# Attention in steps of four scores and about four maxima, each followed by a batch with V of at most four banks

## The reference

```python
t = _to_tokens(x)                      # 16 x 3136 x 32
Q, K, V = ln(t) @ W_Q, ln(t) @ W_K, ln(t) @ W_V
scores = einsum('bqd,bkd->bqk', Q, K) * 32 ** -0.5
probs = softmax(where(causal, scores, -inf), axis=-1)
t = t + einsum('bqk,bkd->bqd', probs, V)
```

## Time and profile before

| | |
|---|---|
| median of three runs (lowest, highest) | 4711.1 us (4706.0, 4712.6) |
| the profiled execution's own time | 4710.3 us |
| its span | 4708.6 us |
| TensorE matmul busy | 4141.0 us (88%), 51290 matmuls |
| VectorE busy | 3134.4 us (67%) |
| ScalarE busy | 2752.3 us (58%) |
| POOL busy | 1430.2 us (30%) |
| mean granted TensorE clock | 0.942 of 2.4 GHz |
| layer 2 attention, first score to end | 1597 to 2984 us |
| layer 3 attention, first score to end | 3168 to 4547 us |

### The profile page before, as it was taken

One profiled execution on the slowest core, in us unless ns is written; L12 is line 12 of the kernel. 1 busy time (PEld: TensorE's weight loads), 2 busy tenths in 40 slices (PEclk: granted clock), 3 DMA queues, 4 the chain that ended last, 5 costly groups with the idle time before them and its releaser, 6 DMA issues. The chain is left out here.

```text
span 4708.6 us, 125775 instructions
## 1 busy us (share of the span) xinstructions
PE 4141.0 (88%) x51290; PEld 2867.8 (61%) x51290; DVE 3134.4 (67%) x6164; ACT 2752.3 (58%) x5706; POOL 1430.2 (30%) x2222
## 2 busy tenths in 40 slices
PE   3888888888686799999999999779999999999975
PEld 2666666666332466666676666456666666666754
DVE  4777777777798466666666666536666666666653
ACT  2777777776586355655655555415555556556541
POOL 4333223321000343433433432122433434334220
PEclk9999999999798699999999999769999999999987
DMA  1200000000000000000000000000000000000003
GB/s 25 33 3 3 2 2 3 2 2 2 3 1 1 1 2 2 2 2 3 2 3 2 2 2 2 6 1 2 2 2 2 3 2 2 2 2 2 3 6 55
DMA packets 348272, 24.07 MB, mean 5 GB/s; under 512 B 346388, under 2 KB 347700, under 8 KB 347700
## 3 DMA queue, kind: packets, MB, share of 16 engines
q1 hardware_dynamic: 347700, 16.03, 4.7%
HBM read 7.88 MB, written 6.42 MB: 3 GB/s over the span
## 5 line engine op out<-in xcount | busy, mean ns | idle before, releaser
L561 DVE TENSOR_REDUCE L2a_mx<-L2a_r 128x1 f32<-128x512 f32 (+4 forms) x1344 | 760.8, 627 | 243.4 <-PE L2a_r L425 240.3
L561 DVE TENSOR_REDUCE L3a_mx<-L3a_r 128x1 f32<-128x512 f32 (+4 forms) x1344 | 760.5, 627 | 239.8 <-PE L3a_r L425 236.4
L529 ACT ACTIVATE L2a_e<-L2a_r 128x512 f32<-128x512 f32 (+3 forms) x1344 | 658.8, 579 | 284.9 <-PE L2a_r L404 282.7
L529 ACT ACTIVATE L3a_e<-L3a_r 128x512 f32<-128x512 f32 (+3 forms) x1344 | 658.6, 579 | 280.5 <-PE L3a_r L404 278.5
L425 PE MATMUL L2a_r<-L2a_vT,L2a_qT 32*128 32x512 f32 (+3 forms) x3488 | 817.6, 529 | 0.0
L425 PE MATMUL L3a_r<-L3a_vT,L3a_qT 32*128 32x512 f32 (+3 forms) x3488 | 815.0, 528 | 0.1
L404 PE MATMUL L2a_r<-L2a_qT,L2a_vT 32*128 32x512 f32 (+4 forms) x3488 | 779.8, 518 | 29.4 <-DMA L2a_qT<-L2a_nm 29.4
L404 PE MATMUL L3a_r<-L3a_qT,L3a_vT 32*128 32x512 f32 (+4 forms) x3488 | 777.6, 516 | 27.3 <-DMA L3a_qT<-L3a_nm 27.3
L1454 POOL TENSOR_SCALAR win_xw<-win_xr,win_mv,win_rs 32x343 f32<-32x343 f32 (+7 forms) x432 | 327.9, 779 | 703.3 <-ACT win_rs L1242 703.2
L404 PEld LDWEIGHTS L2a_r<-L2a_qT,L2a_vT 32*128 32x128 f32 x3488 | 372.1, 188 | 189.3 <-issue 100.3
L404 PEld LDWEIGHTS L3a_r<-L3a_qT,L3a_vT 32*128 32x128 f32 x3488 | 370.6, 187 | 186.8 <-issue 98.9
(11 more groups left out here) (370 smaller groups left out, 6745.0 us busy)
## 6 DMA issues: line engine op xcount, KB each, us to landing
L2a_qT<-L2a_nm SPq DMA_DIRECT2D x768, 0.5 KB, 2.0
L3a_qT<-L3a_nm SPq DMA_DIRECT2D x768, 0.5 KB, 2.0
T<-in_x SPq DMA_DIRECT2D x16, 384.0 KB, 3.7
out<-T SPq DMA_DIRECT2D x16, 384.0 KB, 4.0
win_mq<-win_nmt SPq DMA_DIRECT2D x256, 3.1 KB, 1.7
win_msk<-in_L_conv_pos_emb SPq DMA_DIRECT2D x49, 0.2 KB
L2a_qT<-L2a_nm SPq DMA_DIRECT2D x32, 0.2 KB, 1.8
L3a_qT<-L3a_nm SPq DMA_DIRECT2D x32, 0.2 KB, 1.8
```

Source lines behind the costliest of these rows:

```text
L529: nc.scalar.activation(E[0:r, n % RE, 0:w], bank_of(x)[0:r, 0:w], ACT.Exp).then_inc(exp_done, 1)
L561: return nc.vector.tensor_reduce(to, frm, AX.X, ALU.max)
```

## The change

LEAD stays, BATCH and the even cuts go. The scores of a block are cut into groups of four (the last one of a block takes the rest; the last block has three and three), and a group is a step. A step holds two scores, two maxima, two scores, two maxima; maxima come into the step in which their old time falls. At the end of the step (END) stands the batch of V of the group of the step before (LAG is now one step), which accumulates at most four banks, and behind it what is due of acc, final, vT and the mask of the next step. q stands after the second pair of scores and maxima and ahead of V. There are 23 groups per image, 368 in all; the accumulators of V that VectorE adds go from 48 to 256 for each layer. The ring keeps its eight banks. vT of the next image is tied to the closing of blocks, and vr moves to a later time. The two semaphores for full banks become two each, one per row group.

```diff
-    LEAD, LAG, BATCH = 28, 6, 12
+    LEAD, GROUP, LAG = 28, 4, 1
...
-            parts = -(-(b - a) // BATCH)
-            cuts = [a + (b - a) * i // parts for i in range(parts + 1)]
-            BATCHES += [(y - 1 + LAG, img, j, x, y) for x, y in zip(cuts, cuts[1:])]
+            cuts = [*range(a, b, GROUP), b] if j < TAIL else [a, a + 3, b]
+            GROUPS += [(img, j, x, y) for x, y in zip(cuts, cuts[1:])]
+    NG = len(GROUPS)
+    GROUP_OF = {n: g for g, (_, _, a, b) in enumerate(GROUPS) for n in range(a, b)}
...
+    STEP = [math.floor(step_of(n * NS / NM - LEAD)) for n in range(NM)]
...
-            spots = [(len(MAXES) + i, x[0]) for i in range(len(banks) + 1) for x in BATCHES
-                     if x[0] // 2 == max_time(len(MAXES) + i) // 2 - 1]
-            spot, at = spots[0] if spots else (len(MAXES), max_time(len(MAXES)) - 2)
+            spots = [i for i in range(len(banks) + 1)
+                     if len(MAXES) + i == 0 or STEP[len(MAXES) + i] > STEP[len(MAXES) + i - 1]]
+            spot = spots[0] if spots else 0
...
+    END = 9
+    timed = [((GROUP_OF[n], (n - GROUPS[GROUP_OF[n]][2]) // 2), ("score", n)) for n in range(NS)]
+    timed += [((STEP[n], NTH[n] // 2), ("max", n)) for n in range(NM)]
+    timed += [((STEP[n] - 1, END), ("mask", n)) for n in MASKED]
+    timed += [((g + LAG, END), ("pv", g)) for g in range(NG)]
+    timed += [((g + LAG, END), ("acc", g)) for g in range(NG)]
+    CLOSE = {}
+    for (img, j), groups in BLOCK_GROUPS.items():
+        CLOSE[img, j] = groups[-1] + LAG + 1
+        timed += [((CLOSE[img, j], END), ("final", img, j))]
...
+            elif img == 1:
+                at = CLOSE[0, max(f - 2, 0)]
             else:
-                at = min((x[0] for x in BATCHES), key=lambda t: abs(t - at))
-            timed += [(at, ("vT", img, f)), (at + 4, ("q", img, f))]
-        vr = (img - 2) * PER + 62 if img > 1 else (img - 1) * PER + 1 if img else -LEAD - 20
+                at = CLOSE[(img - 2, NJ - 2 + f) if f < 2 else (img - 1, f - 2)]
+            timed += [((at, END), ("vT", img, f)), ((at + 1, 1), ("q", img, f))]
+        vr = (img - 2) * PER + 76 if img > 1 else (img - 1) * PER + 1 if img else -LEAD - 20
...
+    WORK = [x for at, x in sorted(timed, key=lambda y: (*y[0], RANK[y[1][0]]))]
...
+    COPY = {x[0]: n for n, x in enumerate(BLOCK_GROUPS.values())}
+    ADD = {g: n for n, g in enumerate(g for g in range(NG) if g not in COPY)}
...
+    S_SIDE = {n: n % 2 for n in range(NS)}
+    S_NTH = {n: n // 2 for n in range(NS)}
+    M_SIDE = {n: n % 2 for n in range(NM)}
+    M_NTH = {n: n // 2 for n in range(NM)}
...
-                        last.then_inc(s_full, 1)
+                        last.then_inc(s_full[S_SIDE[n]], 1)
...
-                        act.wait_ge(s_full, n + 1)
+                        act.wait_ge(s_full[S_SIDE[n]], S_NTH[n] + 1)
...
-                        dve.wait_ge(m_full, n + 1)
+                        dve.wait_ge(m_full[M_SIDE[n]], M_NTH[n] + 1)
```

More of the change, by code:

```diff
@@ L150, in causal_attention @@
[L150 to L153, removed]
-    for img in range(NB):
[L155 to L159, removed]
+            spots = [i for i in range(len(banks) + 1)
+                     if len(MAXES) + i == 0 or STEP[len(MAXES) + i] > STEP[len(MAXES) + i - 1]]
@@ new lines, in causal_attention @@
+            spot = spots[0] if spots else 0
+            MASKED.add(len(MAXES) + spot)
+            banks.insert(spot, ("edge", 0))
+            MAXES += [(img, j, x) for x in banks]
+    NTH = [n - STEP.index(STEP[n]) for n in range(NM)]
+    RANK = {"score": 0, "max": 1, "q": 2, "pv": 3, "acc": 4, "final": 5, "vT": 6, "mask": 7, "rs": 8, "ors": 9,
+            "res": 10, "out": 11, "vr": 12, "v": 13}
+    END = 9
+    timed = [((GROUP_OF[n], (n - GROUPS[GROUP_OF[n]][2]) // 2), ("score", n)) for n in range(NS)]
@@ L168, in causal_attention @@
         v = (img - 1) * PER + 14 if img > 1 else vr
-        timed += [(vr - 19, ("res", img)), (vr - 7, ("rs", img)), (vr, ("vr", img)), (v, ("v", img))]
+        timed += [(moment(vr - 19), ("res", img)), (moment(vr - 7), ("rs", img)), (moment(vr), ("vr", img)),
+                  (moment(v), ("v", img))]
         out = (img + 1) * PER + 28
-        timed += [(out, ("out", img)), (out + 14, ("ors", img))]
-    WORK = [x for at, x in sorted(timed, key=lambda y: (y[0] // 2, RANK[y[1][0]], y[0]))]
@@ L175, in causal_attention @@
-    BANKED = [x for x in WORK if x[0] in ("mask", "score", "vT", "q", "pv", "final") or x[0] == "max" and x[1] not in MASK_AT]
+        timed += [(moment(out), ("out", img)), (moment(out + 14), ("ors", img))]
+    WORK = [x for at, x in sorted(timed, key=lambda y: (*y[0], RANK[y[1][0]]))]
+    BANKED = [x for x in WORK if x[0] in ("mask", "score", "vT", "q", "pv", "final") or x[0] == "max" and x[1] not in MASKED]
     PLACE = {x: n for n, x in enumerate(BANKED)}
@@ L179, in causal_attention @@
     FINAL = {x: n for n, x in enumerate(y for y in WORK if y[0] == "final")}
-    COPY = {x[1:]: n for n, x in enumerate(y for y in WORK if y[0] == "acc" and y[3] == score_at(*y[1:3]))}
-    ADD = {x[1:]: n for n, x in enumerate(y for y in WORK if y[0] == "acc" and y[1:] not in COPY)}
-    assert [x[:2] for x in COPY] == [x[1:] for x in FINAL]
+    COPY = {x[0]: n for n, x in enumerate(BLOCK_GROUPS.values())}
+    ADD = {g: n for n, g in enumerate(g for g in range(NG) if g not in COPY)}
+    assert [x[1:] for x in FINAL] == list(BLOCK_GROUPS)
     STAT = {x: n for n, x in enumerate(y for y in WORK if y[0] in ("res", "out"))}
@@ L225, in bank_of @@
             if x[0] == "acc":
-                x = ("pv", *x[1:])
-            return R[PLACE[("mask", x[1]) if x[0] == "max" and x[1] in MASK_AT else x] % RING]
+                x = ("pv", x[1])
+            return R[PLACE[("mask", x[1]) if x[0] == "max" and x[1] in MASKED else x] % RING]
         w_in, w_mm, w_zero, w_out = sem("w_in"), sem("w_mm"), sem("w_zero"), sem("w_out")
@@ L272, in causal_attention @@
         stat_step, var_ready, log_ready, root_ready = sem("stat_step"), sem("var_ready"), sem("log_ready"), sem("root_ready")
-        s_full, exp_done, mask_done, pv_done = sem("s_full"), sem("exp_done"), sem("mask_done"), sem("pv_done")
-        m_full, max_read, block_max, shift_in = sem("m_full"), sem("max_read"), sem("block_max"), sem("shift_in")
+        exp_done, mask_done, pv_done = sem("exp_done"), sem("mask_done"), sem("pv_done")
+        s_full = [sem(f"s_full{i}") for i in range(2)]
+        m_full = [sem(f"m_full{i}") for i in range(2)]
+        max_read, block_max, shift_in = sem("max_read"), sem("block_max"), sem("shift_in")
         item_full, item_copied, ot_ready = sem("item_full"), sem("item_copied"), sem("ot_ready")
@@ L417, in _ @@
                         img, j, (part, d) = MAXES[n]
-                        if n not in MASK_AT:
+                        if n not in MASKED:
                             bank_free(x)
@@ L445, in _ @@
                             last = dots(0, q0, d * QB, d * QB + QB)
-                        last.then_inc(m_full, 1)
+                        last.then_inc(m_full[M_SIDE[n]], 1)
                     elif kind == "vT":
@@ L469, in _ @@
                         pe.wait_ge(acc_copied, FINAL[x] + 1)
-                        added = [n for y, n in ADD.items() if y[:2] == (img, j)]
-                        if added:
-                            pe.wait_ge(acc_added, added[-1] + 1)
+                        if BLOCK_GROUPS[img, j][-1] in ADD:
+                            pe.wait_ge(acc_added, ADD[BLOCK_GROUPS[img, j][-1]] + 1)
                         if j < TAIL:
@@ L530, in _ @@
                     elif kind == "acc":
-                        _, img, j, n0, n1 = x
-                        if x[1:] not in COPY:
+                        if x[1] not in COPY:
                             continue
-                        n = COPY[x[1:]]
+                        img, j, n0, n1 = GROUPS[x[1]]
+                        n = COPY[x[1]]
                         w = min(width(j), P)
@@ L587, in _ @@
                                                         AX.X, ALU.max, negate=True).then_inc(block_max, 1)
-                    elif x[0] == "acc" and x[1:] in ADD:
-                        _, img, j, n0, n1 = x
+                    elif x[0] == "acc" and x[1] in ADD:
+                        img, j, n0, n1 = GROUPS[x[1]]
                         n = FINAL[("final", img, j)]
```

42 lines of the change are left out of this document (25 added, 17 removed).

## The result

The changed kernel takes 5018.7 us (median; 5015.3 to 5026.3), the kernel before, on the same chip, 4710.6: a ratio of 1.0658 [1.0639, 1.0676]. It is 308 us slower, where 4653 (58 us faster) was forecast. The profiled execution has a span of 5013.6 us against 4708.6, and a mean granted clock of 0.904 against 0.942.

What follows compares the result with a forecast made beforehand. Bound: VectorE's pace through the ring of eight banks alternating with TensorE's under V. From 4710.3 us, -43 (inner images), +2 (masks), -16 (last images) gave 4653 us; range 4580 to 4725, forecast's chance 0.58.

Steps and rivals of the forecast that it cites:

- Steps and rhythm: Inner image's 23 steps, priced from 2.7 to 4.9 us each: sum 84.8 us, against 85.6 before.
- the plain step: Four scores, maxima, then V of the step before: V starts at 1.91 us, whole step 2.94 us.
- The first image's wait behind POOL: Image 0, V behind POOL's vr and v, 3.06 us before: +1 us net a layer.
- The shift: TensorE's 1.87 us DMA wait per image where block 5 starts: claimed to go in the new order.
- 11.4 needed, no wait: Block 5 starts 14.4 us after step 12 starts; 11.4 us needed, so TensorE does not wait for the DMA.
- With it should go most images at 0.96: Inner images: the slow clock follows the DMA wait at block 5, so most go with it.
- The prediction's 7.3 from the reduction's end to the matmul: Block 5's start: eight small DMAs issued in 5.8 us, 7.3 us from end of reduction to matmul.
- The clock as a rival: Drains and short holes lower TensorE's clock in all 28 inner images: 78 us, 4731 us; chance 0.14.
- two slots: Last block's three-score steps; a slot is two banks of scores and two of maxima at once, 1.46 us there.
- the gain of the rhythm: Inner image, 84.8 against 85.6 us: about 14 us of waiting go, 4.7 for switches and 3.4 for slots come.
- The last image: Each layer's last image, first exponential to end: 74 us instead of 82.0, 8 us a layer.

Runs made afterwards that it cites:

- a_lead36: The changed kernel with maxima running 36 scores ahead instead of 28, nothing else: 4788.2 us, ratio 1.0167 to the kernel before.
- b_lead25: The kernel before with maxima only 25 scores ahead instead of 28: 4862.7 us, ratio 1.0321.
- b_lead36: The kernel before with maxima 36 scores ahead instead of 28: 4598.8 us, ratio 0.9756.
- a_fill: The changed kernel with fourteen extra bf16 matmuls, their result overwritten, ahead of block 5's first score: 5010.2 us, ratio 1.0627.

## Why the prediction was wrong

**Steps and rhythm: right step by step, 1.5 us short in the sum.** V after 1.93 us, the plain step 2.94. In after, the middle value of each of the 23 steps at full clock, from first score to first score in the 28 inner images, is within 0.2 us of the forecast in 20 of them. Outside are step 15 with the wait, and the last block's two: 4.35 and 5.24 for 3.8 and 4.9. They add up to 89.1, or 86.3 without the 2.8 of wait, against 84.8. That a_lead36 has just 84.8 is in part luck: the maxima stand in other steps there, step 14 takes 4.07 in place of 3.1 and step 16 3.05 in place of 4.9. The first image's wait behind POOL, +1 us forecast, went from 3.06 to 4.2.

**The shift: the step that failed.** The prediction read block 5's last maximum 4.0 us into step 12, some ten us before block 5 starts, and concluded "11.4 needed, no wait". It is read at the end of step 14, and from there to where block 5 would start (4054.89 to 4059.2, the mask's start and 0.31) are 4.3 us for the 7.5 needed. In before the same stretch was 7.6-1.87 = 5.7. LEAD is counted in scores, and the time between a maximum and a score depends on what else stands between them. In before these were three scores and, ahead of them, 3.2 us of other matmuls:

```profile
2342.97 2.39 PE L502 MATMUL L2a_r<-L2a_e,L2a_v 128*32 128x128 f32 x68
2345.29 0.49 PE L475 MATMUL L2a_r<-L2a_wfb,L2a_o 128*128 128x132 f32 x2
2345.62 0.60 PE L455 MATMUL L2a_r<-ident,L2a_vr 128*128 128x128 f32 x4
...
2346.18 0.70 PE L404 MATMUL L2a_r<-L2a_qT,L2a_vT 32*128 32x512 f32 x2
```

In after they are three scores, two batches of V with 32 matmuls (about 1 us each) and two masks. The wait did not go: it grew from 57 us to 91 in the two layers. "With it should go most images at 0.96" had the link right and the sign wrong: half clock there went from 34 to 198 us, and b_lead25, a_lead36 and b_lead36 move both together. (The prediction's 7.3 from the reduction's end to the matmul is 7.4 by its own rows; nothing hangs on that.)

**The clock as a rival: right in kind, too small by far.** It was priced from the earlier trace rows at 2.8 us an image, and "these falls sit at long waits, not at switches" counted against it. Of the 403 us of new half clock 242 begin at the last block's narrow score matmuls, without a wait, in stretches of 3.4 to 20.5 us. No inner image of before has one there, and there all six scores had one batch of V behind them; cutting them into three and three was taken for two slots, and no more.

**The base of comparison.** Even with the shift mended no gain was there. The 84.8 without a wait was compared with 85.6, which holds one of 1.87 (the prediction says so), and the gain of the rhythm came out as 0.8 us. With LEAD at 36 in both, the old rhythm takes 82.7. The new one is slower by 2.1, of which 1.3 is the split of the last block (84.8 to 83.5) and 0.8 the rest, which the runs do not divide between half-empty slots, q and the switches.

**The sum of the profiled executions** (5013.6-4708.6 = 305 us). More half clock: (529-126)x0.45 = 181. More waiting for the shift: 91-57 = 34. Slower rhythm at LEAD 28: 86.3 against 83.5 (the 13 inner images of before without half clock take 85.3 in the mean, less 1.8 of wait), 28x2.8 = 78. Together 293. The same working for after against a_lead36: 317 us less at half clock are 143, 91 of waits, 28x(86.3-84.8) = 42, together 276. From first score to end the two layers are 268 shorter, and the whole execution 247, as the longer lead puts some 20 us more ahead of the first scores (the first one of layer 2 at 1610.2 in place of 1601.2 us).

**The last image**, 74 forecast, has 28 us at half clock (13 us of time) and a wait of 3.5: 89.4-13-3.5 = 73, so its work was not underestimated. But the 82.0 with which it was compared has 13.7 at half clock (6 us) and a wait of 2.3 as well: 74 too. The 8 us that it was to win a layer were the clock and the wait of before.

Open: what in the last block's two steps brings the clock down, and why the falls last 3.4 us in one image and 13.7 in the next, with the same order of work; why q at the other place and the fillers at block 5 bring more of them.

## What to carry to other kernels

A lead that is counted in items is a time only as long as the rhythm stays: when the order of work is rebuilt, take the real list, find the producer of each late value in it and the consumer, and count the microseconds between them. Compare a forecast without a stall with the old time without its stall; here mending the lead alone was worth 2.4%, and the new rhythm less than nothing. And price a stall of TensorE with the clock that it brings along: here 34 us of added waiting came with 164 us at half clock, 74 us of time.

## What the runs showed of the hardware

- A microsecond at 1.2 GHz cost 0.45 us of this kernel's time, close to the 0.5 that it would be if TensorE set the pace in all of it.
- TensorE can be busy without a gap and still lose its clock: 3.20 of 3.20 us with a matmul in flight, 28 of the 42 with 64 columns, and then 13.6 us at 0.50.
- A wait of 3 us filled with bf16 matmuls of 512 columns (0.22 us apart) kept the clock at 1.00 (a_fill; 17 us of half clock at block 5 in place of 198); the same wait left empty was followed by 1.3 us of work at 1.00 and then 10.2 us at 0.50.
- 83.0 us for 23 batches of V an image against 82.7 for ten: going between matmuls on 32 rows and on 128 cost 0.3 us net for 13 round trips.
